# A six-layer network on one core: the expert layer entered batch by batch, and its third weight unit split by VectorE

## What is computed

```python
# the last step of the phase layer: y (2, 128, 768), then  x = x + y @ W_out
y = (y_val * jax.nn.silu(y_gate)).reshape(b, l, -1)
return y @ W_out

# the experts, on _layernorm(x): E, K, I, SI = 16, 4, 176, 704
router_logits = x @ gate_w.T
routing_probs = jax.nn.softmax(router_logits, axis=-1)
topk_w, topk_idx = jax.lax.top_k(routing_probs, K)
topk_w = topk_w / topk_w.sum(axis=-1, keepdims=True)
combine = (one_hot(topk_idx, E) * topk_w[..., None]).sum(1)
shared = _silu_mul(x @ shared_gate_up.T, SI) @ shared_down.T
shared = shared * jax.nn.sigmoid(x @ shared_gate_vec.T)
for w_gu, w_d, cw in experts:                 # 16 of them, all computed
    h = silu(x @ w_gu[:I].T) * (x @ w_gu[I:].T)
    acc = acc + h @ w_d.T * cw[:, None]
return shared + acc
```

## Time and profile before

| | us |
|---|---|
| median of 3 runs (427.44 to 428.08) | 427.47 |
| the profiled execution | 426.43 |
| its span, first to last instruction | 424.5 |
| PE busy (share of the span) | 392.1 (92%) |
| DVE | 300.9 (71%) |
| ACT | 265.3 (62%) |
| POOL | 205.9 (48%) |
| mean granted TensorE clock | 0.992 |

### The profile page before, as it was taken

One profiled execution on the slowest core, in us unless ns is written; L12 is line 12 of the kernel. 1 busy time (PEld: TensorE's weight loads), 2 busy tenths in 40 slices (PEclk: granted clock), 3 DMA queues, 4 the chain that ended last, 5 costly groups with the idle time before them and its releaser, 6 DMA issues.

```text
span 424.5 us, 14332 instructions
## 1 busy us (share of the span) xinstructions
PE 392.1 (92%) x6016; PEld 327.9 (77%) x6016; DVE 300.9 (71%) x681; ACT 265.3 (62%) x547; POOL 205.9 (48%) x255
## 2 busy tenths in 40 slices
PE   7979999999999999888999988799789998999996
PEld 4656767777667777678999986678678887989995
DVE  6688989997888877757988886677896657222220
ACT  2467878888888888965465534524998235545531
POOL 2467756676567665005546501410498536445430
PEclk9989999999999999999999999999999999999999
DMA  4096641542311100460000052210000580000000
GB/s 158 6 330 224 222 138 46 183 148 75 111 35 38 32 26 5 152 273 2 0 2 1 2 220 121 72 66 2 3 2 0 204 349 0 2 1 2 0 2 25
DMA packets 10831, 34.77 MB, mean 82 GB/s; under 512 B 2192, under 2 KB 7312, under 8 KB 8976
## 3 DMA queue, kind: packets, MB, share of 16 engines
q1 hardware_dynamic: 10480, 33.08, 22.4%
q10 hardware_dynamic: 288, 0.79, 0.5%
HBM read 33.60 MB, written 0.26 MB: 80 GB/s over the span
## 4 chain that ended last, share of the span: by engine, by line
PE 68%; DVE 17%; POOL 6%; issue 4%; ACT 3%; DMA 1%; SPq 0%; DVEq 0%; POOLq 0%; ACTq 0%
PE ps L1668 9%; PE ps L1623 8%; PE ps L1146 8%; PE ps L1132 6%; PE ps L406 5%; PE ps L1655 3%; PE ps L1638 3%; PE ps L392 3%; PE ps L467 3%; PE ps L875 2%; PE ps L857 2%; PE ps L816 2%; PE ps L823 2%; PE ps L352 2%; PE ps L435 1%
## 5 line engine op out<-in xcount | busy, mean ns | idle before, releaser
L1589 ACT ACTIVATE sb_arena<-ps 128x1024 f32<-128x1024 f32 x128 | 123.5, 1020 | 21.9 <-PE ps L1655 21.8
L1668 PE MATMUL ps<-sb_arena 128*25 128x128 f32 (+1 forms) x2048 | 69.4, 276 | 0.8 <-issue 0.6
L1668 PEld LDWEIGHTS ps<-sb_arena 128*25 128x25 f32 (+1 forms) x2048 | 50.7, 98 | 8.4 <-issue 1.2
L1623 PE MATMUL ps<-sb_halves 128*128 128x512 f32 x192 | 54.6, 420 | 1.7 <-DVE sb_arena L1394 1.0
L1178 POOL TENSOR_TENSOR sb_halves<-sb_big,sb_halves 128x704 fp32r<-128x704 f32 x20 | 33.7, 1690 | 38.7 <-ACT sb_halves L1172 38.7
L1244 DVE SCALAR_TENSOR_TENSOR sb_arena<-ps,sb_w_q,sb_arena 128x176 f32<-128x176 f32 x40 | 15.9, 400 | 42.7 <-ACT sb_arena L1196 42.5
L1623 PEld LDWEIGHTS ps<-sb_halves 128*128 128x128 f32 x192 | 34.6, 193 | 14.5 <-issue 6.2
L1146 PE MATMUL ps<-sb_halves 128*128 128x352 f32 x240 | 42.9, 332 | 2.0 <-POOL sb_halves L1178 2.0
L496 POOL TENSOR_TENSOR sb_halves<-sb_big,sb_halves 128x256 fp32r<-128x256 f32 x28 | 21.1, 773 | 45.3 <-ACT sb_halves L480 45.3
L1483 POOL TENSOR_TENSOR sb_big<-sb_arena 128x256 f32<-128x256 f32 x31 | 19.0, 614 | 49.1 <-DVE sb_arena L1355 49.1
L1146 PEld LDWEIGHTS ps<-sb_halves 128*128 128x128 f32 x240 | 39.1, 189 | 3.3 <-DVE sb_arena L1244 1.7
(11 more groups left out here) (234 smaller groups left out, 836.9 us busy)
## 6 DMA issues: line engine op xcount, KB each, us to landing
sb_arena<-in_ctx SPq DMA_DIRECT2D x32, 128.0 KB, 2.1
sb_mid<-in_w_down SPq DMA_DIRECT2D x1, 3584.0 KB, 11.3
sb_big<-in_w_gu SPq DMA_DIRECT2D x1, 3520.0 KB, 12.0
sb_mid<-in_w_ffn SPq DMA_DIRECT2D x3, 768.0 KB, 4.4
sb_big<-in_w_gu SPq DMA_DIRECT2D x1, 2112.0 KB, 7.7
sb_big<-in_w_q SPq DMA_DIRECT2D x2, 1024.0 KB, 5.7
sb_big<-in_w_k SPq DMA_DIRECT2D x2, 1024.0 KB, 5.5
sb_big<-in_w_v SPq DMA_DIRECT2D x2, 1024.0 KB, 5.8
```

The costliest lines, as they stand in the source:

```text
L1589: nc.scalar.activation(probs[:, n % P_SLOTS].rearrange("p a g n -> p a (g n)"), ps[:, bank:bank + 2], ACT.Exp, scale=XD ** -0.5).then_inc( ...
L1623: i = T.matmul(ps[:, 7], ctx_half[:, t % 2, c, kt], wkv_half[:, d, kt], start=(n + kt == 0), stop=(n == 2 and kt == KT - 1))
L1668: i = T.matmul(ps[32 * gg:32 * gg + m, 6, j * P:(j + 1) * P], v_sb[:, t % V_SLOTS, 4 * gg + j, head], probs[:, n % P_SLOTS, a, gg], start= ...
```

## The change

Five edits, all around the entry of the experts.

1. **Phase output by batch**: the last four half steps of `sum_y` are written (1, batch 0), (2, batch 0), (1, batch 1), (2, batch 1).
2. **Entry by batch**: `layer_norm`, `ln_copy` and `split_x` are not used here any more. Batch 0 is added, normalised, turned and split ahead of batch 1; the batches have banks 0 and 6. There are 6 warming products in place of 24.
3. **Router behind the first product**: the logits are formed after k0; batch 1 is turned inside k0, ahead of its last two instructions.
4. **Third unit on DVE**: DVE rounds and subtracts the weights of unit 2, ahead of the gating of k0; ACT and POOL leave that unit out.
5. Some semaphores are merged (`shared_exp` and `routes_exp`, `lg_shifted` into `logits_taken`, `ones_set` and `zeros_set`), with no change in what waits for what.

```diff
-        WARM = {0: 20, 1: 24, 2: 24, 5: 58, 6: 24}
+        WARM = {0: 20, 1: 24, 2: 24, 5: 58, 6: 6}
...
-            sum_y(1)
-            sum_y(2)
+            sum_y(1, 0)
+            sum_y(2, 0)
+            sum_y(1, 1)
+            sum_y(2, 1)
...
         def tensor_experts(pe):
             T = nc.tensor
-            ln_transpose(pe, LN_OF["moe"], 0)
-            pe.wait_ge(sem("xnT_ready"), 4)
-            pe.wait_ge(sem("w_moe"), loaded["w_moe"])
-            for b in range(B):
+            keep_warm(WARM[LN_OF["moe"]], 0)
+
+            def turn_x(b):
+                pe.wait_ge(sem("ln_normed"), B * LN_OF["summary2"] + b + 1)
+                for kt in range(KT):
+                    i = T.transpose(ps[:, 6 * b, kt * P:(kt + 1) * P], xn[:, b, kt * P:(kt + 1) * P], id32[:])
+                i.then_inc(sem("ln_transposed"), 1)
+
+            def route(b):
+
+                pe.wait_ge(sem("xnT_ready"), 4 + b)
+                pe.wait_ge(sem("w_moe"), loaded["w_moe"])
                 for kt in range(KT):
                     i = T.matmul(ps[:, 1, b * 32:b * 32 + 17], xnT[:, kt, b, 3:], w_rt[:, kt], start=(kt == 0),
                                  stop=(kt == KT - 1))
-            i.then_inc(sem("routed"), 1)
+                i.then_inc(sem("routed"), 1)
+
+            turn_x(0)
...
-                if b == 0:
-                    pe.wait_ge(sem("gu_low"), u + 1)
+                if b == 0 and u == 2:
+                    pe.wait_ge(sem("third_low"), 1)
+                elif b == 0:
+                    pe.wait_ge(sem("gu_low"), u + 1 - (u > 2))
                 for n, (d, c) in enumerate(HALF_PRODUCTS):
-                    if k == 0 and n != 1:
-                        pe.wait_ge(sem(("xe_high", None, "xe_low")[n]), 1)
+                    if k < B and n != 1:
+                        pe.wait_ge(sem(("xe_high", None, "xe_low")[n]), k + 1)
+                    if k == 0 and n == 2:
+                        turn_x(1)
...
                 i.then_inc(sem("gu_projected"), 1)
+                if k == 0:
+                    for b in range(B):
+                        route(b)
+                    b = 0
...
             for u in range(UNITS):
-                pool.wait_ge(sem("gu_high"), u + 1)
+                if u == 2:
+                    continue
+                pool.wait_ge(sem("gu_high"), u + 1 - (u > 2))
...
-                    if u + 2 < UNITS:
+                    if 0 < u < UNITS - 2:
                         unit_high(act, u + 2)
...
-            layer_norm(dve, LN_OF["moe"], add_previous)
-            ln_copy(dve, 5, 0)
-            split_x(dve, xe_half, 0, "xe")
-            dve.wait_ge(sem("routed"), 1)
+            stats(0)
+            aggregate(0)
+            normalise(0)
+            stats(1)
+            aggregate(1)
+            high(0)
+            low(0)
+            normalise(1)
+            whole(0)
+            high(1)
+            whole(1)
+            low(1)
+            dve.wait_ge(sem("routed"), B)
...
+            dve.wait_ge(sem("gu_loaded"), 16 * 3)
+            dve.wait_ge(sem("gu_projected"), B)
+            V.tensor_copy(gu_half[:, 0, 0], unit_weights(2)).then_inc(sem("third_high"), 1)
+            dve.wait_ge(sem("third_high"), 1)
+            V.tensor_tensor(gu_half[:, 0, 1], unit_weights(2), gu_half[:, 0, 0].bitcast(F32), ALU.subtract
+                            ).then_inc(sem("third_low"), 1)
```

More of the change, by code:

```diff
@@ L880, in tensor_phase, with sum_y @@
                     turn_y(0)
-            def sum_y(t):
+            def sum_y(t, b):
                 pe.wait_ge(sem("yT_taken"), t + 1)
-                for b in range(B):
[L885 to L888, removed]
+                for u in range(2 * t, 2 * t + 2):
+                    i = T.matmul(ps[:, 3 + b, 0:D], yT[:, u, b * P:b * P + P], w_out2[:, u], start=(u == 0), stop=(u == 5))
+                if t == 2:
+                    i.then_inc(sem("phase_out"), 1)
             pe.wait_ge(sem("y_gated"), 3 * B)
@@ L1186, in scalar_experts @@
             act.wait_ge(sem("logits_taken"), 1)
-            nc.scalar.activation(ex[:, :, 16:17], lg[:, :, 16:17], ACT.Exp, scale=-1.0).then_inc(sem("shared_exp"), 1)
-            act.wait_ge(sem("lg_shifted"), 1)
-            nc.scalar.activation(ex[:, :, 0:16], ex[:, :, 0:16], ACT.Exp).then_inc(sem("routes_exp"), 1)
+            nc.scalar.activation(ex[:, :, 16:17], lg[:, :, 16:17], ACT.Exp, scale=-1.0).then_inc(sem("route_exp"), 1)
+            act.wait_ge(sem("logits_taken"), 2)
+            nc.scalar.activation(ex[:, :, 0:16], ex[:, :, 0:16], ACT.Exp).then_inc(sem("route_exp"), 1)
             nc.scalar.preload_act_table_set("silu_and_others")
@@ L1222, in vector_experts, with stats, aggregate, normalise @@
             V = nc.vector
-            layer_norm(dve, LN_OF["moe"], add_previous)
-            ln_copy(dve, 5, 0)
-            split_x(dve, xe_half, 0, "xe")
-            dve.wait_ge(sem("routed"), 1)
+            def stats(b):
+                add_previous(b)
+                step(dve, V.bn_stats(bn[:, b], x[:, b]))
+            def aggregate(b):
+                V.bn_aggr(mv[:, b], bn[:, b]).then_inc(sem("ln_stats"), 1)
+            def normalise(b):
+                dve.wait_ge(sem("ln_rstd"), B * LN_OF["moe"] + b + 1)
+                V.tensor_scalar(xn[:, b], x[:, b], mv[:, b, 0:1], rstd[:, b:b + 1], ALU.subtract, ALU.mult
+                                ).then_inc(sem("ln_normed"), 1)
+            def turned(b):
+                return ps[:, 6 * b, 0:256].rearrange("p (k l) -> p k l", k=KT)
+            def high(b):
+                dve.wait_ge(sem("ln_transposed"), 6 + b)
+                V.tensor_copy(xe_half[:, 0, :, b * P:b * P + P], turned(b)).then_inc(sem("xe_high"), 1)
+            def low(b):
+                dve.wait_ge(sem("xe_high"), b + 1)
+                V.tensor_tensor(xe_half[:, 1, :, b * P:b * P + P], turned(b), xe_half[:, 0, :, b * P:b * P + P].bitcast(F32),
+                                ALU.subtract).then_inc(sem("xe_low"), 1)
+            def whole(b):
+                V.tensor_copy(xnT[:, :, b, 3:], turned(b)).then_inc(sem("xnT_ready"), 1)
+            stats(0)
[11 more added lines that the diff above has]
+            dve.wait_ge(sem("routed"), B)
             V.tensor_copy(lg, ps[:, 1, 0:64].rearrange("p (b n) -> p b n", b=B)[:, :, 0:17]).then_inc(sem("logits_taken"), 1)
@@ L1695, in _ @@
                     project(0)
-            pe.wait_ge(sem("zeros_set"), 1)
+            pe.wait_ge(sem("constants_set"), 2)
             keep_warm(4, 6)
```

15 lines of the change are left out of this document (7 added, 8 removed).

## The result

The changed kernel takes 423.95 us (median of 6 runs, 423.50 to 425.13) against 427.61 us for the kernel before (6 runs, 427.10 to 428.08): ratio 0.9924, 95% interval 0.9908 to 0.9940. Two later comparisons gave 424.79 against 426.95 (ratio 0.9953, 0.9936 to 0.9971) and 424.50 against 427.20 (0.9945, 0.9926 to 0.9964).

A forecast was written before the change was run, and what follows sets the result against it. TensorE was taken as the bound, with 68% of the chain of waits and back-to-back work from k8 on. The median 427.47 less 2.0 us gained up to k8 gave 425.5 us, range 424.8 to 426.7.

The forecast's parts named there:

- k0: First of the experts' forty gate/up products, two per unit, one per batch, numbered from 0 to 39; forecast start 345.57.
- k8: First gate/up product of the fifth unit; forecast to start at 356.65 instead of 358.65, 2.0 us ahead.
- The chain to k8: From the phase layer's last product into the experts: all waits up to k8 together shorten by 2.0 us.
- POOL's hold on the normalisation: Batch 0's normalisation on DVE waits for POOL's split of the second unit, ending at 344.03, not 343.55.
- rival (a): Batch 0's normalisation isn't held up by POOL; the chain up to k8 moves by 0.5, giving 425.0; chance 0.12.
- The router instruction under POOL's fifth split: A small DVE router instruction falls into POOL's split of the fifth unit and holds back a gating to 356.6.
- The new wait ahead of k6: TensorE waits 0.85 us for the fourth unit's weights, now the first that ACT and POOL deliver.
- (b): Slower rounding, costlier steps or another router instruction under a POOL split lose 0.4 to 1.0: 425.9 to 426.5; chance 0.15.
- (c): TensorE's clock falls once after little work from 343.95 to 347.6, losing 1.7: 427.2, no difference; chance 0.07.
- (d): TensorE's clock falls already in the entry's first wait and stays low for 7 us, costing 3.5: 429.0; chance 0.06.
- (e): The change does nothing since the fifth unit's weights hold k8; the prediction rejected it and gave no chance.
- The sum: Whole execution: median 427.47 less 2.0 gives 425.5 us, the 2.0 staying up to the end.

The follow-up runs named there:

- `mask_later`: The changed kernel with some of VectorE's small router instructions moved behind a later gating, out of POOL's split of the fifth unit: 423.78 us, ratio 0.9933 to before.
- the case of 120 memsets: The changed kernel with 120 one-column memsets on VectorE, ten behind each of twelve gatings from k8 on: 424.65 us in one execution.
- `both`: The changed kernel with POOL's split of the second unit held until batch 0 is normalised, plus the edit of `mask_later`: 423.56 us, ratio 0.9928 to before.

## Why the prediction was wrong in size and right in its steps up to k8

Step by step, with 0.29 added to the changed kernel's times to put its anchor at that of before:

| step | predicted | measured |
|---|---|---|
| DVE's first addition | 341.57 | 341.71 |
| normalisation of batch 0 ends | 344.03 | 344.02 |
| k0 | 345.57 | 345.48 |
| k1 | 348.07 | 347.99 |
| logits taken | 348.3 | 348.18 |
| third unit split on DVE | 349.41, 0.52 + 0.89 | 349.35, 0.53 + 0.89 |
| k4 | 351.3 | 351.21 |
| k6, and its wait for POOL | 354.1, 0.85 | 354.09, 0.68 |
| k8 | 356.65 | 356.76 |
| k8 to the last addition | 61.9 | 61.9 |

- **The chain to k8: right.** 2.0 us predicted, 1.89 measured. The largest miss is at the first addition, which came 0.67 us earlier: of the 0.86 for four instructions less, 0.19 was lost to the order in which the copied pieces are needed, where I had allowed 0.05.
- **POOL's hold on the normalisation: right.** It ended 0.15 behind POOL's split, and removing the overlap gave back 0.30 of k8. I had priced rival (a) at 0.5; 0.2 of that was not to be had, as batch 0 itself came 0.17 later than I had reckoned.
- **The router instruction under POOL's fifth split: right**, and it was what set k8 (0.30 by `mask_later`), just ahead of TensorE itself.
- **The new wait ahead of k6: right**, 0.68 for 0.85.
- **Rivals (b), (c), (d)**: none moved k8 as priced. The rounding took 0.53. But a second router instruction did land under a POOL split, as (b) feared: L1319 took 1.30 us, to just behind the end of the fourth unit's split (353.65). In the kernel before it took 0.65, also to just behind a split's end. TensorE was waiting for that same split, and what the longer DVE row cost further on wasn't tried. The clock stayed at 1.00, and TensorE was busy 2.48 us in the stretch for which (c) had reckoned 1.9 to 2.2. (e) is refuted by k8.
- **The sum: this step failed.** It was made as 427.47 - 2.0 with the words that the 2.0 us stay up to the end, and took the 1.93 us around the span and everything behind the last addition as they were. The store and the program's end shrank from 5.42 to 4.77: the term was sized 0 and measured -0.65. With it the forecast is 427.47 - 1.89 + 0.03 - 0.65 = 424.96. That lies inside the stated range, so this term explains the shift of the traces and not the whole of the miss. My reading of the trace left out the DMA view of the last 4 us; the instruction packet stood in it. What follows from changing DVE's count by five (681 to 686) could have been named as a rival there, though not its sign without a run.
- **What is left.** 424.96 is within 0.5 of the two later comparisons (424.79 and 424.50), and is 1.0 above the first (423.95). The traced pieces give -2.51 without what lies ahead of the anchor; the three comparisons gave -3.66, -2.16 and -2.70. In the three traces of the changed kernel the time behind the anchor is the same, 84.81 to 84.86 us; what varies is the stretch ahead of it (338.81 to 340.07). The kernel before, too, has had medians from 426.68 to 427.61 in its comparisons. I take the 1.0 us to be of that kind: a low draw for the one and a high draw for the other. That isn't shown for those runs, and the cause of the variation is open. The range had no room for it: its lower end was (a) less 0.2.

## What to carry to other kernels

Two edits that remove consecutive waits are to be priced together along the chain: alone they were worth 0.11 and 1.00 us, together 1.89. Where the trace shows a DVE instruction of the same kind held by POOL (here a TENSOR_SCALAR and a CAST within SBUF, and a TENSOR_TENSOR with both inputs there), price it by POOL's end, and then look whether one of the two can be moved: two such reorderings gave another 0.59 us at k8. And when a change of 0.5% or less is judged, cut the execution at a point that the change doesn't touch and look at the last DMA by itself, since a single added instruction can move the end by 0.7 us.

## What the runs showed of the hardware that I had not expected

- One packet of instructions (8 KB, queue 14) that falls among the 272 packets of the final store delays its landing from 2.2 to 2.9 us, though the store takes only 20 to 30% of the 16 engines' time in the windows shown; seven packets straggle in the kernel before. Where it falls follows VectorE's number of instructions, in two pairs that are 128 apart (681 and 809, 683 and 811), and hangs on a single one.
- With the packet absent the span ends 2.54 to 2.58 or 2.83 to 2.89 us after the store's issue, but what lies around the span makes up for it (2.18 to 2.23 against 1.80 to 1.86, the case of 120 memsets left aside): 423.63 - 421.4 in the changed kernel and 423.86 - 422.0 in `both`. So a comparison of spans alone would have told of 0.3 us that aren't there; the end is to be taken against the execution's own time.
